# Convolution block on one core: output sum in column tiles, row products in row tiles

## What is computed

```
x = x + conv_ref(group_norm(x), ...)             # stage 1
t = tokens(x)
t = t + attention(layer_norm(t), ...)            # stage 2
t = t + ffn(layer_norm(t), ...)                  # stage 3

def conv_ref(x, qkv_w, proj_w, proj_b, ln_g, ln_b, fc1_w, fc1_b, fc2_w, fc2_b):
    xs  = tokens(x)                              # B, 1024, 96
    xn  = layer_norm(xs) * ln_g + ln_b
    mid = silu(xn @ fc1_w + fc1_b) @ fc2_w + fc2_b
    q, k, v = split(xs @ qkv_w)                  # 8 heads of 12
    q, k = q / |q|, k / |k|
    attn = k^T v                                 # per head
    o = 0.5 * v + 1 / pi * q @ attn
    o = o / |o| + mid
    return o @ proj_w + proj_b                   # turned back to channels x pixels
```

## Time and profile before

| | |
|---|---|
| time, median of 3 runs | 2901.9 us (2897.7 to 2904.84) |
| profiled execution | span 2901.5 us; the page gives no other time of it |
| TensorE busy | 2730.6 us, 94% of the span |
| VectorE busy | 2300.3 us, 79% |
| ScalarE busy | 2020.8 us, 70% |
| GpSimd busy | 1153.0 us, 40% |
| DMA | 316.04 MB, mean 109 GB/s |

### The profile page before, as it was taken

The page is one execution under the profiler, slowest core; times in us unless marked ns, Lnnn a source line. Parts: engine busy times, 40 slices in busy tenths (PEclk is TensorE's granted clock), DMA queues, the critical chain, the costliest instruction groups (busy, mean ns, idle before and its releaser), DMA issues. The chain is left out here.

```text
span 2901.5 us, 86028 instructions
## 1 busy us (share of the span) xinstructions
PE 2730.6 (94%) x28924; PEld 1685.7 (58%) x29306; DVE 2300.3 (79%) x4585; ACT 2020.8 (70%) x3943; POOL 1153.0 (40%) x1999
## 2 busy tenths in 40 slices
PE   4999999999999499999999999999999997899996
PEld 2555555555554266666666666666666664455553
DVE  3577676676765499999999999999999994678997
ACT  2677777777776267777777777777777774577775
POOL 1144443444434434444444444444444441224445
PEclk9999999999999699999999999999999998999998
DMA  1113223232332466666666666666666663334555
GB/s 34 44 55 115 90 100 114 76 114 85 105 114 85 128 118 119 116 118 118 118 118 118 118 118 118 118 117 117 117 117 117 118 117 86 99 105 132 147 142 154
DMA packets 923408, 316.04 MB, mean 109 GB/s; under 512 B 848785, under 2 KB 906418, under 8 KB 923314
## 3 DMA queue, kind: packets, MB, share of 16 engines
q1 hardware_dynamic: 921970, 313.59, 47.8%
q10 hardware_dynamic: 1344, 1.18, 0.1%
HBM read 113.35 MB, written 99.88 MB: 73 GB/s over the span
## 5 line engine op out<-in xcount | busy, mean ns | idle before, releaser
L982 DVE TENSOR_REDUCE at_unit_max<-at_ps_queries 128x1 f32<-128x512 f32 (+4 forms) x2304 | 1135.9, 550 | 86.0 <-PE at_ps_queries L853 83.5
L928 ACT ACTIVATE at_probs<-at_ps_keys 128x512 f32<-128x512 f32 x1344 | 743.3, 603 | 388.9 <-PE at_ps_keys L868 384.5
L853 PE MATMUL at_ps_queries<-at_turned 96*128 96x128 bf16 (+3 forms) x3456 | 635.1, 275 | 30.6 <-DMA at_turned<-at_spread 29.4
L868 PE MATMUL at_ps_keys<-at_turned 128*128 128x128 bf16 x3453 | 648.4, 275 | 13.3 <-ACT at_probs L928 1.7
L803 POOL TENSOR_TENSOR at_v<-at_stacks,at_one 128x128 f32<-128x128 f32 x192 | 76.7, 399 | 818.5 <-DMA at_stacks<-qkv_rows 818.5
L888 PE MATMUL at_ps_values<-at_probs,at_v 128*32 128x128 f32 x10752 | 373.4, 276 | 6.5 <-ACT at_probs L928 6.5
L868 PEld LDWEIGHTS at_ps_keys<-at_turned 128*128 128x128 bf16 x3456 | 238.0, 97 | 239.5 <-ACT at_probs L928 88.3
L853 PEld LDWEIGHTS at_ps_queries<-at_turned 96*128 96x128 bf16 x3456 | 289.7, 98 | 122.0 <-DMA at_turned<-at_spread 31.3
L888 PEld LDWEIGHTS at_ps_values<-at_probs,at_v 128*32 128x32 f32 x10752 | 269.5, 109 | 120.6 <-ACT at_diag_probs L928 70.2
L928 ACT ACTIVATE at_diag_probs<-at_ps_keys 128x512 f32<-128x512 f32 x384 | 208.7, 595 | 8.5 <-PE at_ps_keys L868 5.6
L822 POOL TENSOR_SCALAR_AFFINE_SELECT at_diag_probs<-at_diag_probs 128x1024 f32<-128x1024 f32 x192 | 210.3, 1095 | 0.0
(11 more groups left out here) (214 smaller groups left out, 4967.4 us busy)
## 6 DMA issues: line engine op xcount, KB each, us to landing
qkv_rows<-cb_packed SPq DMA_DIRECT2D x32, 1536.0 KB, 8.3
at_stacks<-qkv_rows SPq DMA_DIRECT2D x192, 256.0 KB, 3.3
cb_x<-in_x_dram SPq DMA_DIRECT2D x32, 384.0 KB, 3.7
cb_x_again<-in_x_dram SPq DMA_DIRECT2D x32, 384.0 KB, 4.5
x_after_conv<-cb_x SPq DMA_DIRECT2D x32, 384.0 KB, 5.0
attention_rows<-at_att SPq DMA_DIRECT2D x384, 32.0 KB, 2.2
ff_att_rows<-attention_rows SPq DMA_DIRECT2D x32, 384.0 KB, 4.5
ff_x<-x_after_conv SPq DMA_DIRECT2D x128, 96.0 KB, 2.4
```

The lines of the kernel that those rows point to most:

```text
L853: mm = pe.matmul(pq[:, u % QBANKS, c0:c0 + n], QT[0:STACK, slot, qb * P:(qb + 1) * P], KT[0:STACK, slot, k0:k0 + n], start=(c0 == 0), stop ...
L868: mm = pe.matmul(pk[:, bank_k, c0:c0 + n * P], KT[:, slot, kb * P:(kb + 1) * P], QT[:, slot, q0 * P:(q0 + n) * P], start=(c0 == 0), stop=True,
L928: act.activation(probs, pk[:, (slot * NU + k) % KBANKS, :], ACT.Exp, scale=scale).then_inc(S["probs"], 1)
L982: dve.tensor_reduce(peaks, scores, AX.X, ALU.max).then_inc(S["unit_max"], 1)
```

## The change

`X1` and `XR` are no longer 96 channels x 1024 tokens. They are laid out by quarters: partition 32 q + c, block b holds channel 32 b + c for the tokens of quarter q, 3 x 256 values per partition.

- The output sum is made in that layout: for each of the three hidden chunks and for the heads, 3 blocks x 4 quarters of products with 32 outputs and 256 tokens (`out_sums`, `out_heads`), 48 products in place of 8.
- The row products read it: for each half j, the 128 tokens at the same place of all four quarters are handled together. `attn_rows(r, j)` issues 3 blocks x 4 quarters of products with 32 contracted rows each, quarter t into bank t of a four-bank area `wide`; 24 products in place of 8. `w_attn` is held four times in 32 partitions and three blocks.
- ScalarE copies and squares four banks with one instruction each, twice per image.
- The order of TensorE's and ScalarE's body changes: see the fences below.
- `XR` is loaded and `X1` is stored in four transfers of 32 partitions each.
- `prepare` makes `w_attn` and `out_bias` in the new layout: three more loads, more products and two more copies.

```diff
-    w["out_bias"] = sb("out_bias", [C, 1])
-    w["w_attn"] = sb("w_attn", [C, 4 * C])
+    w["out_bias"] = sb("out_bias", [P, 3])
+    w["w_attn"] = sb("w_attn", [P, 3, 4 * C])
...
+        ] + [(projb[q * QP:(q + 1) * QP, :], A["L0_conv_proj_b"].rearrange("(b c) -> c b", c=QP)) for q in range(4)]
...
+                link(dve.tensor_copy(w["w_attn"][:, 1, :], bank[3][:, 0:4 * C]))
+                link(dve.tensor_copy(w["w_attn"][:, 2, :], bank[4][:, 0:4 * C]))
...
+                def attn_rows(ps, b):
+
+                    for q in range(4):
+                        mm = pe.matmul(ps[q * QP:(q + 1) * QP, 0:4 * C], w["centre"][:, b * QP:(b + 1) * QP],
+                                       attn_raw[:, :], start=True, stop=True)
+                    return mm
+
+                for b in range(3):
+                    for q in range(4):
+                        pe.matmul(bank[4][q * QP:(q + 1) * QP, b:b + 1], w["proj"][:, b * QP:(b + 1) * QP], fc2b[:, :],
+                                  start=True, stop=True)
+                attn_rows(bank[5], 0)
...
+                attn_rows(bank[3], 1)
+                attn_rows(bank[4], 2).then_inc(products, 1)
...
-        XR = sb("x_again", [C, 2, L])
-        X1 = sb("x1", [C, 2, L])
+        XR = sb("x_again", [P, 2, 3, QT])
+        X1 = sb("x1", [P, 2, 3, QT])
...
-        pq, pt, pf, po = (ctx.enter_context(nc.psum_tensor("cb_ps_" + n, [P, 2 * BANK], FP32))
-                          for n in ("qkv", "turn", "hidden", "out"))
+        wide = ctx.enter_context(nc.psum_tensor("cb_ps_wide", [P, 4, BANK], FP32))
+        flat = wide[:, :, :].rearrange("p a n -> p (a n)")
+        pq, pt = flat[:, 0:2 * BANK], flat[:, 2 * BANK:4 * BANK]
+        pf, po = (ctx.enter_context(nc.psum_tensor("cb_ps_" + n, [P, 2 * BANK], FP32)) for n in ("hidden", "out"))
...
-                        sp.dma_start(XR[:, (r + 1) % 2, :], x_in[i - 3]).then_inc(xr_loaded[(r + 1) % 2], 16)
+                        for q in range(4):
+                            sp.dma_start(XR[q * QP:(q + 1) * QP, (r + 1) % 2, :, :], quarters(x_in[i - 3])[q]
+                                         ).then_inc(xr_loaded[(r + 1) % 2], 16)
                     if on(4):
                         sp.wait_ge(S["x1_ready"], i - 3)
-                        sp.dma_start(x1[i - 4], X1[:, r, :]).then_inc(x1_stored[r], 16)
+                        for q in range(4):
+                            sp.dma_start(quarters(x1[i - 4])[q], X1[q * QP:(q + 1) * QP, r, :, :]
+                                         ).then_inc(x1_stored[r], 16)
...
-                        dve.wait_ge(xr_loaded[q], _dmas(lap, r, 3, 2))
-                        _above(dve.wait_ge, x1_stored[q], _dmas(lap, r, 5, 2))
-                        _above(dve.wait_ge, S["a_psum"], TILES * (i - 4))
-                        dve.scalar_tensor_tensor(out=X1[:, q, :], in0=po[0:C, :], scalar=w["out_bias"][:, 0:1],
-                                                 in1=XR[:, q, :], op0=ALU.add, op1=ALU.add).then_inc(S["x1_ready"], 1)
+                        dve.wait_ge(xr_loaded[q], 4 * _dmas(lap, r, 3, 2))
+                        _above(dve.wait_ge, x1_stored[q], 4 * _dmas(lap, r, 5, 2))
+                        _above(dve.wait_ge, S["a_psum"], 2 * (i - 4))
+                        for b in range(3):
+                            ins = dve.scalar_tensor_tensor(out=X1[:, q, b, :], in0=po[:, b * QT:(b + 1) * QT],
+                                                           scalar=w["out_bias"][:, b:b + 1], in1=XR[:, q, b, :],
+                                                           op0=ALU.add, op1=ALU.add)
+                        ins.then_inc(S["x1_ready"], 1)
...
+                def silu(i, r, k):
+                    for a in range(2):
+                        act.wait_ge(S["fc1_psum"], 6 * (i - 2) + 2 * k + a + 1)
+                        act.activation(HT[:, r, k, a * BANK:(a + 1) * BANK], pf[:, a * BANK:(a + 1) * BANK],
+                                       ACT.Silu, bias=w["fc1_bias"][:, k:k + 1]).then_inc(S["hid_ready"], 1)
+
+                def copy_rows(i, r, j):
+                    act.wait_ge(S["a_psum"], 2 * (i - 4) + j + 1)
+                    act.activation(AQKV[:, r, j::2, :], wide[:, :, 0:3 * C], ACT.Copy)
+                    act.activation(ASQ[:, j::2, :], wide[:, :, 3 * C:4 * C], ACT.Square).then_inc(S["a_copied"], 1)
...
-                        for k in range(CHUNKS):
-                            for a in range(2):
-                                act.wait_ge(S["fc1_psum"], 6 * (i - 2) + 2 * k + a + 1)
-                                act.activation(HT[:, r, k, a * BANK:(a + 1) * BANK], pf[:, a * BANK:(a + 1) * BANK],
-                                               ACT.Silu, bias=w["fc1_bias"][:, k:k + 1]).then_inc(S["hid_ready"], 1)
+                        silu(i, r, 0)
                     if on(4):
-                        for t in range(TILES):
-                            act.wait_ge(S["a_psum"], TILES * (i - 4) + t + 1)
-                            if t == 0:
-                                _above(act.wait_ge, S["v_ready"], i - 5)
-                                _above(act.wait_ge, S["a_sums"], i - 4)
-                            act.activation(AQKV[:, r, t, :], second_ps(t)[:, 0:3 * C], ACT.Copy)
-                            act.activation(ASQ[:, t, :], second_ps(t)[:, 3 * C:4 * C],
-                                           ACT.Square).then_inc(S["a_copied"], 1)
+                        _above(act.wait_ge, S["v_ready"], i - 5)
+                        _above(act.wait_ge, S["a_sums"], i - 4)
+                        copy_rows(i, r, 0)
+                    if on(2):
+                        silu(i, r, 1)
+                        silu(i, r, 2)
+                    if on(4):
+                        copy_rows(i, r, 1)
...
+                def out_sums(q, k):
+                    for b in range(3):
+                        for t in range(4):
+                            pe.matmul(po[t * QP:(t + 1) * QP, b * QT:(b + 1) * QT], w["fc2"][:, k, b * QP:(b + 1) * QP],
+                                      HT[:, q, k, t * QT:(t + 1) * QT], start=(k == 0 and b != 1), stop=False,
+                                      skip_group_check=True)
+
+                def out_heads():
+                    for b in range(3):
+                        for t in range(4):
+                            mm = pe.matmul(po[t * QP:(t + 1) * QP, b * QT:(b + 1) * QT],
+                                           w["proj"][:, b * QP:(b + 1) * QP], OHT[:, t * QT:(t + 1) * QT], start=False,
+                                           stop=True, skip_group_check=True)
+                    return mm
+
+                def attn_rows(r, j):
+                    for b in range(3):
+                        for t in range(4):
+                            rows = slice(t * QP, (t + 1) * QP)
+                            mm = pe.matmul(wide[:, t, 0:4 * C], X1[rows, r, b, j * P:(j + 1) * P],
+                                           w["w_attn"][rows, b, :], start=(b == 0), stop=(b == 2))
+                    mm.then_inc(S["a_psum"], 1)
...
-                        for a in range(2):
-                            half = slice(a * BANK, (a + 1) * BANK)
-                            for k in range(CHUNKS):
-                                pe.matmul(po[0:C, half], w["fc2"][:, k, :], HT[:, q, k, half], start=(k == 0),
-                                          stop=False)
-                            if a == 0:
-                                pe.wait_ge(S["oht_ready"], i - 2)
-                            mm = pe.matmul(po[0:C, half], w["proj"][:, :], OHT[:, half], start=False, stop=True)
-                        mm.then_inc(S["out_done"], 1)
-                    if on(2):
-                        hidden(i, 1)
-                        hidden(i, 2)
+                        out_sums(q, 0)
+                        out_sums(q, 1)
                     if on(4):
                         if on(3):
                             pe.wait_ge(S["oht_ready"], i - 2)
                         if on(1):
                             pe.wait_ge(S["qkv_copied"], 8 * i)
-                        for t in range(TILES):
-                            if t >= 4:
-                                pe.wait_ge(S["a_copied"], 8 * (i - 4) + t - 3)
-                            elif on(5) and not on(1):
-                                pe.wait_ge(S["a_copied"], 8 * (i - 5) + t + 5)
-                            pe.matmul(second_ps(t), X1[:, r, t * P:(t + 1) * P],
-                                      w["w_attn"][:, :], start=True, stop=True).then_inc(S["a_psum"], 1)
+                        if on(5):
+                            pe.wait_ge(S["a_copied"], 2 * (i - 4))
+                        attn_rows(r, 0)
+                    if on(2):
+                        hidden(i, 1)
+                    if on(3):
+                        out_sums(q, 2)
+                        pe.wait_ge(S["oht_ready"], i - 2)
```

(6 more changed lines are left out.)

31 lines of the change are left out of this document (13 added, 18 removed).

## The result

The changed kernel takes **2921.06 us** (median of 4 runs, 2916.76 to 2928.04), the kernel before 2900.31 us beside it (4 runs, 2897.7 to 2904.84): ratio 1.0071, 95% interval 1.0055 to 1.0088. It is slower by more than the 0.3% that can be told from no change. The prediction was 2884 us with a range of 2866 to 2915, and faster as the likeliest case: wrong in sign and outside its range.

A forecast was written before the change was run, and what follows sets the result against it. TensorE bounds the kernel, with a VectorE and ScalarE chain to the Silu almost as long. 2901.5 - 17 (28 steady bodies) - 6.5 (six end bodies) + 6.3 (preparation) = 2884 us; eight in ten from 2866 to 2915.

The forecast's parts named there:

- late rows: Steady bodies: packed rows landing later cost 0.2 us per body; rival, a microsecond later still, 2906 us, chance 0.10.
- The second path through VectorE and ScalarE: Steady body: chain from L615 through VectorE's reductions, roots and Silu, with PE only 0.29 us behind it.
- PE would wait 1.9 us (1.6) before hidden product 1: After the first row section PE waits for the Silu, so 1.9 us of the saving becomes idle time.
- 0.27 us won in front of it: Part of a body's 0.8 us gain that lies before hidden product 1; 0.54 lies behind it.
- row groups that load and run side by side: Row products: four row groups overlap, 3.87 us instead of 5.16; rival, loads in turn, 2904 us, chance 0.13.
- The preparation: Before the bodies: added loads, products and copies lie wholly on the path, 6.3 us lost, within 5 to 9.
- entering and leaving a tiled section costs 0.13: TensorE's tiled sections: 0.13 us each, four per body with one pair adjacent, about 0.5 us.
- The rival of the clock: Clock falls behind the new wait, 1.6 us each: half the bodies 2906 us (chance 0.12), every body 2929 (0.07).
- the point of decision: Clock falls over the bodies: from 11 falls on, their 1.6 us losses decide against the net 17.5 us gain.
- six bodies at the two ends: 6.5 won: Bodies lacking some stages: between 0 and 2.5 us gained each, 0 to 15 in all, 6.5 taken.
- the bodies around it repeat the picture: Bodies around the one read show the same near-tie of PE and chain; only the transfer's landing moves.
- SyncE's queue: Eight pieces delay the packed rows' store by 2.6 us, up to 3.2; 0.2 us per body taken.

The follow-up runs named there:

- Experiments 1 and 2: Changed kernel with four, then two, added products of 256 columns in TensorE's wait before hidden product 1: 2910.4 us (1.0030), then 2912.3 us (1.0036).
- experiments 7 and 8: Changed kernel with packed rows stored ahead of the eight pieces: 2967.9 us; the same with GpSimd's product waiting for VectorE's subtraction: 2903.3 us.

## Why the prediction was wrong

The forecast gained 17.0 us and the trace lost 17.7. By the table, 18.0 of these 34.7 us lie in the bodies at the two ends and behind them, 12.8 in the quiet body and 8.2 in the clock of bodies 7 to 30; late rows and the last stages give 4.2 back.

**What held.** The second path through VectorE and ScalarE; that PE would wait 1.9 us (1.6) before hidden product 1 and that this product would start at 17.2 us; 0.27 us won in front of it; row groups that load and run side by side. In the steady bodies the copies on ScalarE cost nothing, and the rows came late in four bodies only. The preparation, 6.3 forecast and 6.2 found, was in part luck: the loads cost 1.8 us instead of 1.3 and the twelve one-column products 0.3 instead of 1.1, and in the nine kernels here with this preparation body 2 starts at 57.2 to 58.6 us, 4.8 to 6.2 later than in the one trace of the kernel before.

**The step "entering and leaving a tiled section costs 0.13".** It was read from the section alone, start of the section to start of what follows. The border also lengthens the untiled product next to it: 1.98 in the second line of the earlier trace rows against 1.88 in the earlier trace rows was that tenth, and I didn't read it. The work from hidden product 1 on without borders is 1.72 + 2.59 + 1.72 + 1.94 + 1.76 = 9.73, the trace has 10.56: 0.83 more, in place of 0.26. About 0.1 of that is the start behind the wait, which the prediction didn't have either; the rest is four borders at 0.18 each, about half of it in the section and half in its neighbour. A quiet body won 0.27 instead of 0.8 us. Over 24 bodies this is 13 us.

**The rival of the clock.** Named, with its price (1.6 us, measured 1.63) and given 0.19 in all. It fell in 9 bodies, below the 11 that I had as the point of decision, but 15 us against a net gain that was itself too large. Experiments 1 and 2 show that the idle time is the cause. Which of the 22 waits of 1.5 to 2.1 us in bodies 7 to 30 end in a fall (four did) stays open.

**The step "six bodies at the two ends: 6.5 won".** They lost, and this is the largest part of the miss. Bodies 4 and 5 did win, 1.44 us each. Body 3 rose from 23.75 to 26.76 us: part of the sum now stands behind the wait, and the clock fell. Bodies 6, 31 and 32 took 29.03 us before and hidden product 1 started there at 18.38, with the Silu as its releaser: PE was already behind the chain, with nothing to win. I had said that "the bodies around it repeat the picture" without looking at these. There the wait grew to 2.8 us and the clock fell in all three (30.6 us).

Behind the last body another 4.2 us went, and here SyncE's queue, priced in the prediction for the steady bodies alone, does arrive. Kernel before, then the change:

```profile
971.77 1.48 ACT L543 ACTIVATE cb_packed<-cb_a_qk 128x1536 bf16<-128x1536 f32 x1 [2.06 <-DVE cb_a_qk L421]
973.75 2.93 PE L656 MATMUL cb_ps_turn<-w_attn,cb_x 96*128 96x384 f32 x4 [3.37 <-ACT cb_a_squares L566]
```

```profile
990.21 1.48 ACT L577 ACTIVATE cb_packed<-cb_a_qk 128x1536 bf16<-128x1536 f32 x1 [5.66 <-DMA qkv_rows<-cb_packed]
993.14 4.08 PE L628 MATMUL cb_ps_wide<-w_attn,cb_x 32*128 32x384 f32 x24 [7.55 <-ACT cb_a_squares L546]
```

The last row section waits for ScalarE's copy and square of the half before it, and these stand behind L577, which waits for the packed rows to land (counted from the start of body 33, 917.76 and 933.43: at 56.8 us, where L543 started at 54.0 and waited for VectorE). Their store is issued at 49.2 us instead of 46.6: it stands behind the four pieces of `X1` (1.8 us of issuing, where one transfer took 0.3), and these start 1.2 us later since they wait for their `X1`. With the rows stored first (experiments 7 and 8) L577 waits for VectorE again, the last row section waits 3.96 us instead of 7.55, and the stretch takes 88.3 and 89.4 us, against 95.1 in the change and 90.9 before.

**Attention and last stage** took 2.2 us less. Their code is the same in all fourteen traces, and there they take 1889.6 to 1892.8 us from the attention's first product to the end: the 2.2 us lie within that spread.

## What to carry to other kernels

Where a second chain is nearly as long as the bounding engine, the saved time must be placed *in front of* that chain's end or the chain must start earlier: the same tiles made the kernel 21 us slower or 43 us faster by the order of their sections. Count borders between tiled and untiled products by their neighbours too, and keep tiled sections together. A wait of 1.6 us that comes in every body can cost more than its length, since the clock may fall behind it; two useless products in it paid. The first and last bodies of a pipeline have other waits than the steady one; read them too before they are given a gain.

## What the runs showed of the hardware

- A transfer that lands *earlier* can slow a kernel by 1.5%: it released GpSimd just ahead of a VectorE subtraction with both inputs in SBUF, which then took 3.02 us instead of 1.75. Where VectorE came first, it was GpSimd's product that took 2.90 us. The place of one semaphore wait on GpSimd was worth some 64 us.
- Twelve products of 32 rows in four row groups take 2.14 us with 384 columns, against 2.58 for four of 96 rows: only 17% less, where the section of the sum gains 21% (2.73 against 3.44).
- How often the granted clock fell went with the length of TensorE's idle time before it. In bodies 4 to 32 of the fourteen traces it fell behind none of 196 waits of up to 1.3 us, behind 15 of 55 of 1.45 to 1.9 us, and behind 25 of 30 of 2.6 us and more (each body by its longest wait).
